# A causal mask moved from a TensorE matmul to a VectorE add, for tiles 4 to 15 of an attention kernel

## What is computed

```python
q = x_norm @ qkv[:, :KEY]
k = x_norm @ qkv[:, KEY:2 * KEY]
v = x_norm @ qkv[:, 2 * KEY:]
scores = jnp.einsum('bsk,btk->bst', q, k) * scale
causal = jnp.tril(jnp.ones((S_len, S_len), dtype=bool))
scores = jnp.where(causal[None], scores, -jnp.inf)
attn = jax.nn.softmax(scores, axis=-1)
out = (attn @ v) @ o_proj + residual
```

## Time and profile before

| what | value |
|---|---|
| median of 3 runs | 1663.91 us (1661.66 to 1664.42) |
| the profiled execution's own time | 1662.27 us |
| its span, first to last instruction | 1660.5 us |
| PE busy | 1626.9 us, 98% of the span, 7615 matmuls |
| DVE busy | 879.6 us, 53%, 2264 instructions |
| ACT busy | 681.2 us, 41% |
| mean granted clock of TensorE | 0.994 |
| mask matmuls (L1296) | 64, between 45.2 us and 1198.1 us of the span |

### The profile page before, as it was taken

One profiled execution on the slowest core, in us unless ns is written; L12 is line 12 of the kernel. 1 busy time (PEld: TensorE's weight loads), 2 busy tenths in 40 slices (PEclk: granted clock), 3 DMA queues, 4 the chain that ended last, 5 costly groups with the idle time before them and its releaser, 6 DMA issues.

```text
span 1660.5 us, 23631 instructions
## 1 busy us (share of the span) xinstructions
PE 1626.9 (98%) x7615; PEld 1344.8 (81%) x7615; DVE 879.6 (53%) x2264; ACT 681.2 (41%) x1301; POOL 284.5 (17%) x491
## 2 busy tenths in 40 slices
PE   9999999899999989999999999999989999999998
PEld 7888888788888878888887788888878888888886
DVE  5464645455364554556455455555555655556553
ACT  5443433353343344343333335333344444454443
POOL 1121101121120112121110112020131212212121
PEclk9999999999999999999999999999999999999999
DMA  4111625321153431124534122253663313133100
GB/s 159 58 64 53 156 78 137 86 93 54 59 139 96 118 105 64 64 89 106 131 88 115 51 83 102 77 137 95 156 135 56 51 25 51 28 48 48 27 0 8
DMA packets 365766, 136.64 MB, mean 82 GB/s; under 512 B 317008, under 2 KB 321104, under 8 KB 365664
## 3 DMA queue, kind: packets, MB, share of 16 engines
q1 hardware_dynamic: 354768, 116.48, 28.2%
q10 hardware_dynamic: 10896, 18.90, 3.4%
HBM read 79.73 MB, written 55.59 MB: 81 GB/s over the span
## 4 chain that ended last, share of the span: by engine, by line
PE 55%; issue 33%; POOL 5%; ACT 3%; DVE 2%; DMA 1%; SPq 0%; POOLq 0%; ACTq 0%; DVEq 0%
PE psum L346 17%; PE psum L348 16%; PE psum L347 16%; POOL rstd L507 2%; ACT tok L633 1%; PE psum L1306 1%; ACT xin L633 1%; PE psum L1242 1%; PE psum L1422 1%; PE psum L1421 1%; PE psum L1414 1%; PE psum L1413 1%; POOL expo L582 1%; POOL shift L509 1%; DVE stats L884 1%
## 5 line engine op out<-in xcount | busy, mean ns | idle before, releaser
L346 PE MATMUL psum<-xt_hi,g_hi 128*128 128x512 f32 (+3 forms) x640 | 237.4, 371 | 0.4 <-DVE g_lo L910 0.4
L348 PE MATMUL psum<-xt_lo,g_hi 128*128 128x512 f32 (+3 forms) x640 | 229.6, 359 | 0.0
L347 PE MATMUL psum<-xt_hi,g_lo 128*128 128x512 f32 (+3 forms) x640 | 229.2, 358 | 0.0
L346 PE MATMUL psum<-v_hi,pt_hi 128*128 128x512 f32 x544 | 222.9, 410 | 4.9 <-DVE tok L952 3.2
L347 PE MATMUL psum<-v_hi,pt_lo 128*128 128x512 f32 x544 | 215.2, 396 | 0.0
L348 PE MATMUL psum<-v_lo,pt_hi 128*128 128x512 f32 x544 | 215.1, 395 | 0.0
L504 POOL TENSOR_TENSOR var_eps<-meanvar,eps 128x2 f32<-128x2 f32 (+1 forms) x97 | 19.3, 199 | 1025.9 <-DVE meanvar L888 1023.6
L933 DVE TENSOR_REDUCE rowmax<-psum 128x1 f32<-128x512 f32 (+3 forms) x160 | 97.0, 607 | 149.1 <-PE psum L348 147.8
L808 ACT ACTIVATE act_f<-psum 128x512 f32<-128x512 f32 x128 | 76.6, 598 | 209.7 <-PE psum L348 209.7
L633 ACT ACTIVATE tok<-tok,shift,rstd 128x512 f32<-128x512 f32 x128 | 97.4, 808 | 99.7 <-POOL shift L509 99.4
L582 POOL TENSOR_TENSOR expo<-euler,shifted 128x32 f32<-128x32 f32 x16 | 86.9, 5432 | 297.8 <-DVE shifted L1145 297.8
(11 more groups left out here) (150 smaller groups left out, 3410.5 us busy)
## 6 DMA issues: line engine op xcount, KB each, us to landing
xin<-in_x ACTq DMA_DIRECT2D x64, 256.0 KB, 2.8
tok<-in_x SPq DMA_DIRECT2D x64, 256.0 KB, 2.7
x_scratch<-tok SPq DMA_DIRECT2D x64, 256.0 KB, 2.2
out_dram<-tok SPq DMA_DIRECT2D x64, 256.0 KB, 2.3
p_scratch<-probs SPq DMA_DIRECT2D x64, 256.0 KB, 2.0
probs<-p_scratch SPq DMA_DIRECT2D x256, 64.0 KB, 2.6
x_in<-x_scratch SPq DMA_DIRECT2D x64, 256.0 KB, 4.1
p_scratch<-probs SPq DMA_DIRECT2D x16, 192.0 KB, 1.9
```

The lines of the kernel that those rows point to most:

```text
L346: pe.matmul(o, ws, ms, start=first, stop=False, skip_group_check=True)
L347: pe.matmul(o, w_lo, ms, start=False, stop=False, skip_group_check=True)
L348: return pe.matmul(o, ws, m_lo_, start=False, stop=last, skip_group_check=True)
```

## The change

The mask of tiles 0 to 3 stays the bfloat16 matmul in PE. For tiles 4 to 15 the matmul is left out, and DVE adds `mask_bf` to the 128 diagonal columns of the last chunk's scores, in place in PSUM, ahead of that chunk's maximum. The add is counted by `own`, so the maximum waits for it.

```diff
-            OWN = PAIRS + TILES + TILES * 3 + (TILES - GROUP)
+            OWN = PAIRS + TILES + TILES * 3 + (TILES - GROUP) + (TILES - GROUP)
...
+            def hide_later_keys(b, t):
+
+                c, w = chunks(t) - 1, width(t, chunks(t) - 1)
+                dve.wait_ge(scores_ready, b * CHUNKS + BEFORE[t] + c + 1)
+                corner = psum[:, c, w - P:w]
+                mine(dve.tensor_tensor(corner, corner, mask_bf[:], ALU.add))
+
             def row_bias(b, t):
 
+                if t >= GROUP:
+                    hide_later_keys(b, t)
                 mine(chunk_max(b, t, chunks(t) - 1))
...
             split_g(0, 0)
+            dve.wait_ge(consts_ready, 3)
             row_bias(0, 0)
...
-                    if k == 0 and c == chunks(t) - 1:
+                    if k == 0 and c == chunks(t) - 1 and t < GROUP:
 
                         pe.matmul(psum[:, c, w - P:w], ident_bf[:], mask_bf[:], start=False, stop=False, skip_group_check=True)
```

## The result

| kernel | runs | median, us (lowest to highest) | profiled execution, us | its span, us |
|---|---|---|---|---|
| before | 7 | 1661.81 (1661.50 to 1664.42) | 1662.27 | 1660.5 |
| changed | 7 | 1670.06 (1668.36 to 1671.33) | 1668.93 | 1667.1 |

The ratio of changed to before is 1.0045, with a 95% interval of 1.0033 to 1.0056: the change makes the kernel slower by 5.5 to 9.3 us, 7.5 us in the middle. The forecast was no change (-1.5 us), and its range ended at 1666.8 us.

What follows compares the result with a forecast made beforehand. The prediction took PE's instruction stream as the bound. Its terms, -3.4 + 1.2 + 0.7 = -1.5 us, gave 1662.4 us against a median of 1663.91 us, counted as no change, with a range of 1659.5 to 1666.8 us.

Steps and rivals of the forecast that it cites:

- the prediction's first: Whole kernel: PE, busy 98% of the span, sets the time; only matmuls dropped and waits for later DVE results change it.
- The sum: Whole kernel: -3.4 us of PE matmuls, +1.2 in tile 8, +0.7 in tiles 3 and 4, together -1.5 us.
- DVE's pause ahead of L884: Tile 3, before the statistics of x: 0.44 us idle in three loop passes, taken to move elsewhere, starting the chain 0.41 earlier.
- The add: On DVE, tiles 4 to 15: 0.28 us each, 0.31 with the start of the dependent maximum.
- The dear add: Rival on DVE's in-place PSUM write: at 0.75 us per add the sum is +3.9 us, 1667.8 us; chance 0.09.
- Tile 8: Every batch: the add lies in a gapless DVE run that PE waits for, 4 x 0.31 = 1.2 us more.
- Tile 12: PE already waits for `pt_lo` here, so the 0.13 us saved turns into waiting and brings nothing.
- Tiles 3 and 4: Adds delay `affine` by 0.18 us and `pt_lo` by 0.31 per batch; with the pause moved, 0.7 us in all.
- The pause ahead of L884 neither stayed nor left: Rival in tile 3: DVE's pause stays, tiles 3 and 4 cost 2.0 us, sum -0.2, 1663.7 us; chance 0.16.
- everything was not hidden: Rival, all tiles: adds fall into DVE's idle time and all 6.2 us go, 1657.7 us; chance 0.13.
- the matmul was not free: Rival on PE: weight loads set the pace, so dropping mask matmuls gains 0; about +2.4 us, 1666.3 us; chance 0.06.
- The slower rival: The dear add, the only rival counted as slower: a slow in-place PSUM write on DVE, 1667.8 us; chance 0.09.

Runs made afterwards that it cites:

- after_shift: The changed kernel with two extra bfloat16 matmuls ahead of everything, so PE's loop starts four instructions later: 1660.92 us, ratio 0.9988 to the kernel before.
- before_shift: The kernel before with 12 warming matmuls in place of 14, so PE's loop starts eight instructions earlier, masks all on PE: 1671.45 us, ratio 1.0046.
- +2 against 0 in the table: Loop start two PE instructions later than in the changed kernel (0): the changed kernel with the mask of tiles 5, 9, 12, 15 back on PE, 1657.77 us.

## Why the prediction was wrong

**The step that failed** is the prediction's first: "PE's stream is the path, and only two things change the time: what PE no longer issues, and where PE comes to wait for a result that DVE now gives later." There is a third: where in its own stream PE's instructions stand. The sum put that at nothing; it measured 9.6 us, in two stalls of 3.62 and 3.04 us and a slower clock behind the first. I had treated fetching as a matter of DVE's pause ahead of L884 and written "No row shows a fetch". The page of before had such a row, q8 with 53 packets; the same view cut to the stretch around a jump shows the packets there. What would have been needed is the question of where the loop's start lies, and the code alone answers only half: that it moves by eight. Where a block ends no row of before said; the one sign was that q8 moves two packets 3 us apart around a jump (449.74 and 452.82 us), with the next ones 14 us ahead and 21 us behind. So a chance for this case could have been given, but not its place.

The Trainium skill, "Runtime: NRT & Kernel Launch", section "Instruction fetch mechanics", which I cited for the pause, has the rule that mattered in a note further down: a taken branch whose target is not in the current window has to fetch it before execution goes on. The traces agree: the branch takes 3.3 to 3.9 us, and within some 5 us of its start q8 moves two packets of 16 kB. The section also calls the cost of a block's end mostly hidden; at 3.62 and 3.04 us behind a jump it was not, with the end right at the target.

**The steps that held**, each beside its row:

- The add. Estimated at 0.28 us; the changed kernel's group by shape has 293 ns. The dear add is out.

```profile
L940 DVE TENSOR_TENSOR psum<-psum,mask_bf 128x128 f32<-128x128 f32 x48 | 14.1, 293 | 15.0 <-PE psum L348 14.6
...
L1306 PE MATMUL psum<-mask_bf,ident_bf 128*128 128x128 bf16 x16 | 3.7, 230 | 0.0
```

- Tile 8. The wait was to grow by 0.44 us and grew from 0.23 to 0.66. The chain is that of the earlier trace rows with L940 in it.
- Tile 12. Its first product was to come 0.13 us later after the last scores; it was 0.20 and is now 0.33:

```profile
565.37 0.28 PE L348 MATMUL psum<-xt_lo,g_hi 128*128 128x256 f32 x1
...
565.70 0.47 PE L346 MATMUL psum<-v_hi,pt_hi 128*128 128x512 f32 x1
```

- Tiles 3 and 4. The pause ahead of L884 shrank from 0.44 us to 0.19, less than the 0.41 taken; the wait for `affine` went from 0.53 to 0.65, and the product of tile 4's second chunk now starts 0.41 behind the matmul before it (406.24, 406.65), where it had stood at 0.23 (407.22, 407.45):

```profile
396.31 1.29 DVE L884 BATCH_NORM_STATS2 stats<-xin 128x6 f32<-128x512 f32 x2 [0.19 <-DVE rinv L954]
...
403.70 0.66 PE L1252 MATMUL psum<-ident,xin 128*128 128x128 f32 x4 [0.65 <-ACT affine L617]
...
406.24 0.39 PE L348 MATMUL psum<-v_lo,pt_hi 128*128 128x512 f32 x1
...
406.65 0.50 PE L346 MATMUL psum<-v_hi,pt_hi 128*128 128x512 f32 x1
```

 From tile 3's first product to tile 5's, after_shift needs 0.36 us more than before in batch 0 and 0.14 to 0.18 in the others, by the starts in the two traces: 0.8 us in all, where the sum had 0.7.
- The sum. With the stalls out of the way (after_shift) the ratio is 0.9988, -2.0 us with an interval of -3.5 to -0.5; the spans differ by 1.9. The forecast was -1.5. So the terms that were in the sum came to the right total, and the missing one was five to six times as large. That the total is so close is in part luck. Measured apart, both halves are larger than in the sum: the matmuls bring 4.1 us (spans) to 6.8 us (ratio) in place of 3.4, and the adds take back 2.2 us (spans) to 4.6 us (medians) in place of 1.9. One miss is the place of tile 4, to which the sum gave no gain: without the mask its first product follows that of tile 3 by 0.13 to 0.27 us less than before, in each of the four batches.

**The rivals.** The pause ahead of L884 neither stayed nor left; everything was not hidden, as tile 8's wait shows; and the matmul was not free, since the kernel without the mask's 48 matmuls is the fastest of all. The slower rival named the add's price and had the sign right for a wrong reason: the add does cost something, but with the stalls gone (after_shift) no loss is left.

What stays open: why the clock fell behind the first stall of the changed kernel and not behind the second, of 3.62 and 3.04 us, when before_shift lost it behind both of its own, 2.80 and 2.97 us.

## What to carry to other kernels

In a kernel with a hardware loop, a change that adds or takes away instructions ahead of the loop's start or in it moves the place of every instruction behind it in the blocks that are fetched; look for idle time put down to "issue" at the first instruction behind a jump and count the packets on the instruction queue there before explaining a small difference by the change itself. Two spare matmuls ahead of the loop tell the two apart: if the idle time behind the jump goes and the time moves by microseconds, the measurement was of the place and not of the work. And where one engine waits for a chain on another, ask for each instance separately whether the moved work lies in front of that wait: here the first products of six tiles came 0.1 to 0.2 us sooner behind the one before, and those of tiles 5 and 9 came 0.1 to 0.4 us later.

## What the runs showed that was not expected

- A jump back to the loop's start takes PE's sequencer 3.3 to 3.9 us in all nine kernels here, and the matmuls still queued cover all of it or all but 0.32 us. A second fetch right behind it is not covered: it cost 2.8 to 3.6 us that no engine's wait explains. Whether it came was decided by two PE instructions among the 1,440 that the trace has ahead of the loop (+2 against 0 in the table, two kernels that also differ in the mask of four tiles).
- A stall of 3.62 us was followed by several us at a granted clock of 1.2 GHz, and together they cost 6.6 us.
